# Two-layer graph attention on one core: the products of the score's last chunk alternated with the first transposes of layer 0

## The chip, the cores and the metric

The kernel runs on one core of one Trainium2 chip (trn2). Its engines are TensorE (PE in the profile; its weight loads are the row PEld), VectorE (DVE), ScalarE (ACT), GpSimd (POOL) and SyncE (SP), which here only issues DMAs. The metric is the device time of one execution in microseconds (us), as the median of several runs.

## What is computed

Layer 0 is a graph attention layer with a rank-one score and a cut, layer 1 a masked attention over fixed keys. Each is followed by a residual and a layer norm. There are 4096 nodes with 128 features, and `adj` is a 4096 x 4096 integer matrix.

```
# layer 0
h = x @ W
e = leaky_relu((h @ a_src)[:, None] + (h @ a_dst)[None, :], 0.2)
valid = (adj > 0) & (h.sum(axis=1) != 0)[None, :]
att = softmax(where(valid, e, -1e9), axis=1); att = where(valid, att, 0)
L = valid.sum(axis=1); top = att.max(axis=1)
attention = where(att >= 1e-4, att, 0) * L[:, None]
attention = where((top > 1e-4)[:, None], attention, 0)
x = layernorm(x + elu(h + attention @ h))
# layer 1
scores = leaky_relu(x @ ks.T, 0.2)
attn = softmax(where(adj > 0, scores, -9e15), axis=1)
out = layernorm(x + attn @ ks)
```

## The kernel before

The 4096 rows are worked off in 32 tiles of 128 rows. A tile's attention matrix is 128 x 4096, cut into four chunks of 1024 columns, and each chunk into eight blocks of 128. The loop is skewed: slot t does layer 0 of tile t and most of layer 1 of tile u = t - 1. There is no scheduler; each engine has its own instruction list written out by hand, in which semaphores (`pe.wait_ge(name, value)`, `.then_inc(name, 1)`) order it against the others.

TensorE's list for one slot (`slot(t)` in the tensor block) is, in this order:

- `score(u, 3)`: the fourth chunk of layer 1's score, six f16 products of 512 columns (lines 286, 287, 291). q and k are split into a high and a low f16 part; for each of the two banks there are high x high, high x low and low x high.
- `turn0(t, 0..3)`: 32 transposes of 128 x 128 f32 (line 211), eight per chunk, of layer 0's attention `att0`. The block of `att0` is the loaded operand, the identity is streamed.
- `sum0(t, 0..3)`: attention @ h, 32 f32 products that the trace shows as 64 matmuls (line 307).
- `turn1(u, 0..3)` and `sum1(u, 0..3)`: the same for layer 1 (lines 211 and 326), with `turn_q(t)` (line 332) between the second and the third sum. It transposes the new x to make q.
- `score(t, 0..2)`: the first three chunks of the next score.

Scores and transposes all go to `work`, a PSUM tensor of three slots of 1024 columns. Chunk c of a score uses slot c % 3, so the fourth uses slot 0 again; `turn0` uses the slots 1, 2, 0, 1. What a slot held must be read out by ScalarE before it is written again:

- `bend1(u, c)` (ScalarE, line 400) reads score chunk c, applies the leaky relu, writes `att1` and counts `bent1`.
- `copy0(t, c)` (ScalarE, line 394) copies the transposed chunk c to `att0T` and counts `copied0`.
- `score(u, 3)` waits for `bent1` of chunk 0 (value 4u + 1). `turn0(t, 0)`, `(t, 1)`, `(t, 2)` wait for `bent1` of chunks 1, 2, 3 (values 4u + 2, 4u + 3, 4u + 4). `turn0(t, 3)` waits for `copied0` of chunk 0. All four also wait for `cut_done`, the count of the cut of layer 0's attention by VectorE (line 516), and name that wait first.

ScalarE's list around this place is `bend1(u, 2)`, `bend1(u, 3)`, `copy0(t, 0..3)`, `raise1(u, 0)` (exponential of layer 1, line 405), `raise0(t + 1, 0)` (line 387), `raise1(u, 1)`, `copy1(u, 0)` (line 412) and on; `bend1(t, 0)` and `bend1(t, 1)` end the slot. VectorE applies the mask to each bent chunk (`mask1`, line 570), takes the row maximum (line 576), builds the next mask (line 477) and does the small steps that lead to the new x (line 561).

Of the kernel before, what the change touches and what calls it, by code (L numbers as in the profile page):

```python
# [5 lines left out]
P = 128  # L6
CHUNK = 1024
BANK = 512
# [19 lines left out]
def graph_layers(nc, x, adj, W, a, ks, out):  # L28
# [4 lines left out]
    CHUNKS = N // CHUNK  # L33
    PER = CHUNK // P
# [8 lines left out]
    with ExitStack() as ctx:  # L43
        def sb(name, shape, dt=F32):
            return ctx.enter_context(nc.sbuf_tensor(name, shape, dt))

        def pair(name, shape, dt=F32):
            return [sb(f"{name}{i}", shape, dt) for i in range(2)]

        def sem(name):  # L50
            return ctx.enter_context(nc.semaphore(name))

        def sem2(name):
# [4 lines left out]
        att0 = pair("att0_", [P, N])  # L58
# [6 lines left out]
        kT = sb("kT", [P, 2, N], F16)  # L65
# [9 lines left out]
        ident = sb("ident", [P, P])  # L75
# [35 lines left out]
        qT = sb("qT", [P, 2, P], F16)  # L111
# [7 lines left out]
        work = ctx.enter_context(nc.psum_tensor("work", [P, SLOTS, CHUNK], F32))  # L119
# [24 lines left out]
        z0_summed, cut0_ready, rz0_ready, cut_done = sem("z0_summed"), sem("cut0_ready"), sem("rz0_ready"), sem("cut_done")  # L144
        edges_ready, gate0_ready, coef0_ready = sem("edges_ready"), sem("gate0_ready"), sem("coef0_ready")
        turned0, copied0, summed0 = sem("turned0"), sem("copied0"), sem("summed0")
# [6 lines left out]
        scored, bent1, masked1, bias1_ready, exp1 = (  # L153
            sem("scored"), sem("bent1"), sem("masked1"), sem("bias1_ready"), sem("exp1"))
# [53 lines left out]
        def _(pe):  # L208
            def turn(n, c, source):
                for b in range(PER):  # L210
                    mm = pe.transpose(work[:, n % SLOTS, b * P:(b + 1) * P], source(c * PER + b), ident[:, :])  # L211
                return mm
# [19 lines left out]
            for c in range(CHUNKS):  # L232
# [4 lines left out]
                for b in range(CHUNK // BANK):  # L237
                    lo = c * CHUNK + b * BANK
                    mm = pe.matmul(work[:, (HT_AT + c) % SLOTS, b * BANK:(b + 1) * BANK], w_sb[:, :],  # L239
                                   xT[:, lo:lo + BANK], start=True, stop=True)  # L240
# [32 lines left out]
            def score(t, c):  # L273
                if c == 0:
                    pe.wait_ge(q_high, t + 1)
                    pe.wait_ge(q_low, t + 1)
                if c == 3:
                    pe.wait_ge(bent1, 4 * t + 1)
                elif t > 0:
                    pe.wait_ge(copied1, 4 * (t - 1) + c + 2)  # L280
                else:
                    pe.wait_ge(copied0, 4)
                for b in range(CHUNK // BANK):
                    part = slice(c * CHUNK + b * BANK, c * CHUNK + (b + 1) * BANK)
                    o = work[:, c % SLOTS, b * BANK:(b + 1) * BANK]
                    pe.matmul(o, qT[:, 0, :], kT[:, 0, part], start=True, stop=False)  # L286
                    pe.matmul(o, qT[:, 0, :], kT[:, 1, part], start=False, stop=False)  # L287
                for b in range(CHUNK // BANK):
                    part = slice(c * CHUNK + b * BANK, c * CHUNK + (b + 1) * BANK)
                    o = work[:, c % SLOTS, b * BANK:(b + 1) * BANK]  # L290
                    mm = pe.matmul(o, qT[:, 1, :], kT[:, 0, part], start=False, stop=True)  # L291
                mm.then_inc(scored, 1)

            def turn0(t, c):
                pe.wait_ge(cut_done, 2 * t + 1 + c // 2)
                if c == 3:
                    pe.wait_ge(copied0, 4 * t + 1)
                elif t > 0:
                    pe.wait_ge(bent1, 4 * (t - 1) + c + 2)
                turn((1, 2, 0, 1)[c], c, lambda b: att0[t % 2][:, b * P:(b + 1) * P]).then_inc(turned0, 1)  # L300

            def sum0(t, c):
                pe.wait_ge(copied0, 4 * t + c + 1)
                if c == 0 and t > 0:
                    pe.wait_ge(y_ready, t)
                for k in range(c * PER, (c + 1) * PER):
                    mm = pe.matmul(acc0, att0T[:, k * P:(k + 1) * P], h_all[:, k, :], start=(k == 0),  # L307
                                   stop=(k == BLOCKS - 1))
                mm.then_inc(summed0, 1)

            def turn1(u, c, layer0):
                pe.wait_ge(exp1, 2 * u + 1 + c // 2)
                if c == 3:
                    pe.wait_ge(copied1, 4 * u + 1)
                elif layer0:
                    pe.wait_ge(copied0, 4 * (u + 1) + c + 2)
                else:
                    pe.wait_ge(bent1, 4 * u + 4)
                turn((2, 0, 1, 2)[c], c, lambda b: att1[:, b * P:(b + 1) * P]).then_inc(turned1, 1)

            def sum1(u, c):
                pe.wait_ge(copied1, 4 * u + c + 1)
                if c == 0 and u > 0:
                    pe.wait_ge(res1_ready, u)
                for k in range(c * PER, (c + 1) * PER):
                    mm = pe.matmul(acc1, att1T[:, k * P:(k + 1) * P], k_all[:, k, :], start=(k == 0),  # L326
                                   stop=(k == BLOCKS - 1))
                mm.then_inc(summed1, 1)

            def turn_q(t):  # L330
                pe.wait_ge(x1_ready, t + 1)
                pe.transpose(qT_ps, x1[t % 2][:, :], ident[:, :]).then_inc(q_turned, 1)

            def slot(t):
                layer0, layer1, u = t < TILES, t > 0, t - 1
                if layer1:
                    score(u, 3)
                if layer0:
                    for c in range(CHUNKS):
                        turn0(t, c)  # L340
                    for c in range(CHUNKS):
                        sum0(t, c)
                if layer1:
                    for c in range(CHUNKS):
                        turn1(u, c, layer0)
                    sum1(u, 0)
                    sum1(u, 1)
                if layer0:
                    turn_q(t)
                if layer1:  # L350
                    sum1(u, 2)
                    sum1(u, 3)
                if layer0:
                    for c in range(3):
                        score(t, c)

            for t in range(TILES + 1):
                slot(t)
# [353 lines left out]
```

## Time and profile before

| | |
|---|---|
| median of 3 runs | 949.72 us (949.38 to 950.56) |
| the profiled execution, its own time | 949.38 us |
| its span in the trace | 947.6 us |
| TensorE's mean granted clock over the span | 0.977 |

One execution was profiled. The span runs from the first to the last instruction of the program; the execution's time is 1.8 us more. In the profile, a group of instructions has its line in the program, its engine, what it writes and reads, how many there are, the time the engine was busy with them and the mean length of one. Matmuls are pipelined: a matmul's record is longer than the distance to the next one, so what a stream of them costs is read from the distances, not from the lengths. The granted clock is 1.00 at 2.4 GHz and 0.50 at 1.2 GHz.

### The profile page before, as it was taken

The numbers are of one execution on the slowest core, as the hardware profiler recorded it, in microseconds if no ns is written. First come the engines' busy times: TensorE is split into PE (matmuls) and PEld (weight loads), VectorE is DVE, ScalarE is ACT, GpSimd is POOL, SyncE is SP. The second block draws the span as 40 slices with busy tenths as digits, with TensorE's granted clock in tenths as the row PEclk, the third lists the DMA queues.
The fourth block names the chain that finished last, engine by engine and source line by source line (L and its number), as shares of the span: only waits on it lengthen the run. The fifth ranks groups of instructions, "written<-read, shape, count | busy, mean of one in ns | idle before, by whom it ended". The sixth has DMA issues, their size and how long they took to land.

```text
span 947.6 us, 17708 instructions
## 1 busy us (share of the span) xinstructions
PE 907.8 (96%) x7152; PEld 802.8 (85%) x7152; DVE 753.2 (79%) x1231; ACT 779.9 (82%) x793; POOL 52.0 (5%) x136
## 2 busy tenths in 40 slices
PE   7954999999999999999999999999999999999996
PEld 4744888888899888888899888888899888888895
DVE  1575888888888898888888898888888898888422
ACT  4345989888898988988898898988898899988754
POOL 0000000000000000000000000000000000000000
PEclk9777999999999999999999999999999999999998
DMA  8204212222222112222222112222222112220000
GB/s 274 68 21 138 93 44 95 95 95 95 96 93 91 48 61 90 95 95 95 96 92 95 56 56 84 95 96 95 95 95 93 67 43 85 95 96 7 4 3 7
DMA packets 19537, 76.70 MB, mean 81 GB/s; under 512 B 1920, under 2 KB 14336, under 8 KB 15360
## 3 DMA queue, kind: packets, MB, share of 16 engines
q1 hardware_dynamic: 19456, 75.57, 22.7%
q8 instruction: 57, 0.93, 0.4%
q14 instruction: 24, 0.20, 0.1%
HBM read 73.47 MB, written 2.10 MB: 80 GB/s over the span
## 4 chain that ended last, share of the span: by engine, by line
PE 92%; DVE 3%; DMA 2%; issue 1%; ACT 1%; SPq 0%; POOL 0%; POOLq 0%; DVEq 0%; ACTq 0%
PE work L211 24%; PE bank L326 24%; PE bank L307 23%; PE work L286 6%; PE work L287 6%; PE work L291 6%; DMA adj_sb<-adj 2%; DVE att L488 1%; PE work L217 1%; PE work L218 1%; PE work L239 1%; DVE adj_sb L483 1%; DMA att<-x 1%; DVE mask L477 0%; ACT att L387 0%
## 5 line engine op out<-in xcount | busy, mean ns | idle before, releaser
L211 PE MATMUL work<-ident,att 128*128 128x128 f32 x2080 | 246.2, 278 | 20.7 <-ACT att0T L394 8.3
L211 PEld LDWEIGHTS work<-ident,att 128*128 128x128 f32 x2080 | 237.1, 143 | 28.4 <-issue 13.9
L326 PE MATMUL bank<-k_all,att1T 128*128 128x128 f32 x2048 | 237.3, 275 | 0.0
L307 PE MATMUL bank<-h_all,att0T 128*128 128x128 f32 x2048 | 235.1, 276 | 0.0
L326 PEld LDWEIGHTS bank<-k_all,att1T 128*128 128x128 f32 x2048 | 233.6, 192 | 0.0
L307 PEld LDWEIGHTS bank<-h_all,att0T 128*128 128x128 f32 x2048 | 232.5, 193 | 0.0
L570 DVE CUSTOM_DVE_ANT_0 att<-att,mask 128x1024 f32<-128x1024 f32 x128 | 156.8, 1225 | 28.0 <-ACT att L400 22.0
L400 ACT ACTIVATE att<-work 128x1024 f32<-128x1024 f32 x128 | 131.1, 1024 | 33.5 <-PE work L291 33.5
L412 ACT COPY att1T<-work 128x1024 f32<-128x1024 f32 x128 | 126.2, 1012 | 30.7 <-PE work L211 30.7
L516 DVE SCALAR_TENSOR_TENSOR att<-att,cut 128x2048 f32<-128x2048 f32 x64 | 147.4, 2345 | 0.0
L488 DVE CUSTOM_DVE_ANT_0 att<-adj_sb,d_all 128x4096 f32<-128x4096 bf16 x32 | 141.6, 4425 | 1.1
L380 ACT ACTIVATE att<-att,s_all 128x4096 f32<-128x4096 f32 x32 | 119.1, 3722 | 14.9 <-DVE top L488 14.9
L405 ACT ACTIVATE att<-att,bias 128x2048 f32<-128x2048 f32 x64 | 130.0, 2033 | 1.5 <-DVE bias L576 1.5
L387 ACT ACTIVATE att<-att,bias 128x2048 f32<-128x2048 f32 x64 | 129.0, 2016 | 0.0
L394 ACT COPY att0T<-work 128x1024 f32<-128x1024 f32 x128 | 120.3, 1036 | 0.3 <-PE work L211 0.3
L286 PE MATMUL work<-kT,qT 128*128 128x512 f16 x256 | 97.8, 382 | 0.7 <-ACT qT L422 0.7
L287 PE MATMUL work<-kT,qT 128*128 128x512 f16 x256 | 97.8, 382 | 0.0
L477 DVE TENSOR_SCALAR mask<-adj_sb 128x4096 bf16<-128x4096 int32 x32 | 73.4, 2294 | 25.5 <-DMA adj_sb<-adj 25.2
L291 PE MATMUL work<-kT,qT 128*128 128x512 f16 x256 | 76.6, 381 | 0.0
L483 DVE TENSOR_TENSOR adj_sb<-mask,zero_cols 128x4096 bf16<-128x4096 bf16 x32 | 73.0, 2283 | 0.0
L291 PEld LDWEIGHTS work<-kT,qT 128*128 128x128 f16 x256 | 25.2, 98 | 30.5 <-issue 0.5
L286 PEld LDWEIGHTS work<-kT,qT 128*128 128x128 f16 x256 | 25.3, 99 | 27.9 <-ACT qT L422 1.0
(69 smaller groups left out, 442.4 us busy)
## 6 DMA issues: line engine op xcount, KB each, us to landing
adj_sb<-adj SPq DMA_DIRECT2D x32, 2048.0 KB, 8.5
att<-x SPq DMA_DIRECT2D x4, 512.0 KB, 5.8
x_sb<-x SPq DMA_DIRECT2D x32, 64.0 KB, 7.4
out<-x SPq DMA_DIRECT2D x32, 64.0 KB, 1.5
w_sb<-W SPq DMA_DIRECT2D x1, 64.0 KB, 3.7
a_sb<-a SPq DMA_DIRECT2D x2, 0.5 KB, 3.6
k_all<-ks SPq DMA_DIRECT2D x1, 0.5 KB, 15.7
```

What stands on the lines that cost most here:

```text
L211: mm = pe.transpose(work[:, n % SLOTS, b * P:(b + 1) * P], source(c * PER + b), ident[:, :])
L286: pe.matmul(o, qT[:, 0, :], kT[:, 0, part], start=True, stop=False)
L287: pe.matmul(o, qT[:, 0, :], kT[:, 1, part], start=False, stop=False)
L291: mm = pe.matmul(o, qT[:, 1, :], kT[:, 0, part], start=False, stop=True)
L307: mm = pe.matmul(acc0, att0T[:, k * P:(k + 1) * P], h_all[:, k, :], start=(k == 0), stop=(k == BLOCKS - 1))
L326: mm = pe.matmul(acc1, att1T[:, k * P:(k + 1) * P], k_all[:, k, :], start=(k == 0), stop=(k == BLOCKS - 1))
L387: nc.scalar.activation(b, b, ACT.Exp, bias=bias0[f % 2][:, :], accum_out=z0[f % 2][:, k:k + 1]).then_inc(exp0, 1)
L400: nc.scalar.activation(att1[:, cols(c)], work[:, c % SLOTS, :], ACT.Prelu, alpha=SLOPE).then_inc(bent1, 1)
L405: nc.scalar.activation(att1[:, half(k)], att1[:, half(k)], ACT.Exp, bias=bias1[u % 2][:, :], accum_out=z1[u % 2][:, k:k + 1]).then_inc(exp ...
L488: nc.vector.tensor_tensor_reduce(att0[p][:, :], mask_and_zero, d_all[:, :], 1.0, -NO_ROW_MAX, ALU.add, ALU.max, top0[p][:, :]).then_inc(ma ...
L516: nc.vector.scalar_tensor_tensor(b, b, cut0[p][:, :], b, ALU.is_ge, ALU.mult).then_inc(cut_done, 1)
L570: nc.vector.tensor_tensor_reduce(att1[:, cols(c)], att1[:, cols(c)], mask[u % MASKS][:, cols(c)], 1.0, -3.0e38, ALU.add, ALU.max, top1[u % ...
```

## The change

In the slots that have both layers (t = 1 to 31), `score(u, 3)` and `turn0(t, 0)` are replaced by one function, `score_and_turn0(u, t)`. It first waits for `bent1` of chunk 1 (4u + 2) and for `cut_done`, and then issues the six products of the score's fourth chunk and the eight transposes of layer 0's first chunk in turn: product, transpose, product, transpose, and after the sixth pair the last two transposes. `scored` is counted by the sixth product, `turned0` by the eighth transpose. Slots, operands and the number of instructions are the same. The first and the last slot, with one layer only, keep the old order.

```diff
+            def score_and_turn0(u, t):
+
+                pe.wait_ge(bent1, 4 * u + 2)
+                pe.wait_ge(cut_done, 2 * t + 1)
+                for i in range(PER):
+                    if i < 4:
+                        b, k_part = i // 2, i % 2
+                        part = slice(3 * CHUNK + b * BANK, 3 * CHUNK + (b + 1) * BANK)
+                        pe.matmul(work[:, 0, b * BANK:(b + 1) * BANK], qT[:, 0, :], kT[:, k_part, part],
+                                  start=(k_part == 0), stop=False)
+                    elif i < 6:
+                        b = i - 4
+                        part = slice(3 * CHUNK + b * BANK, 3 * CHUNK + (b + 1) * BANK)
+                        mm = pe.matmul(work[:, 0, b * BANK:(b + 1) * BANK], qT[:, 1, :], kT[:, 0, part],
+                                       start=False, stop=True)
+                        if b == 1:
+                            mm.then_inc(scored, 1)
+                    mm = pe.transpose(work[:, 1, i * P:(i + 1) * P], att0[t % 2][:, i * P:(i + 1) * P], ident[:, :])
+                mm.then_inc(turned0, 1)
+
             def slot(t):
                 layer0, layer1, u = t < TILES, t > 0, t - 1
-                if layer1:
+                if layer1 and layer0:
+                    score_and_turn0(u, t)
+                elif layer1:
                     score(u, 3)
-                if layer0:
-                    for c in range(CHUNKS):
+                else:
+                    turn0(t, 0)
+                if layer0:
+                    for c in range(1, CHUNKS):
                         turn0(t, c)
                     for c in range(CHUNKS):
                         sum0(t, c)
```

TensorE's list before, from the last products of the score's third chunk to the end of `turn0` (L286, L287 and L291 are the score's products, L211 the transposes, `att_0` the buffer of layer 0's attention; the names in brackets are the semaphores waited for):

```order
142 L291 MATMUL work<-kT,qT 128x512 x2
143 L211 MATMUL work<-ident,att_0 128x128 [waits bent1,cut_done]
144 L211 MATMUL work<-ident,att_0 128x128 x7
145 L211 MATMUL work<-ident,att_0 128x128 [waits bent1,cut_done]
146 L211 MATMUL work<-ident,att_0 128x128 x7
147 L211 MATMUL work<-ident,att_0 128x128 [waits bent1,cut_done]
148 L211 MATMUL work<-ident,att_0 128x128 x7
149 L211 MATMUL work<-ident,att_0 128x128 [waits copied0,cut_done]
150 L211 MATMUL work<-ident,att_0 128x128 x7
```

Row 142 ends the fourth chunk of the score; the four chunks of transposes stand behind it, each with a wait at its first instruction. The same place of the changed kernel (L310 and L315 are now the fourth chunk's products, L319 the transposes between them):

```order
143 L310 MATMUL work<-kT,qT 128x512 [waits cut_done,bent1]
144 L319 MATMUL work<-ident,att_0 128x128
145 L310 MATMUL work<-kT,qT 128x512
...
151 L315 MATMUL work<-kT,qT 128x512
152 L319 MATMUL work<-ident,att_0 128x128
153 L315 MATMUL work<-kT,qT 128x512
154 L319 MATMUL work<-ident,att_0 128x128 x3
155 L211 MATMUL work<-ident,att_0 128x128 [waits bent1,cut_done]
156 L211 MATMUL work<-ident,att_0 128x128 x7
157 L211 MATMUL work<-ident,att_0 128x128 [waits bent1,cut_done]
158 L211 MATMUL work<-ident,att_0 128x128 x7
159 L211 MATMUL work<-ident,att_0 128x128 [waits copied0,cut_done]
160 L211 MATMUL work<-ident,att_0 128x128 x7
```

The score's last product (row 153) now has five transposes ahead of it that stood behind it, and the wait for `bent1` of chunk 1 stands ahead of the fourth chunk's first product. The lists of the other engines are the same as before.

## Rows read from the trace of the kernel before

**Rows 1.** The page: the span, busy engines, and the chain that ended last.
```profile
span 947.6 us, 17708 instructions
PE 907.8 (96%) x7152; PEld 802.8 (85%) x7152; DVE 753.2 (79%) x1231; ACT 779.9 (82%) x793; POOL 52.0 (5%) x136
PE 92%; DVE 3%; DMA 2%; issue 1%; ACT 1%; SPq 0%; POOL 0%; POOLq 0%; DVEq 0%; ACTq 0%
```

**Rows 2.** Busy time by stage: stretch, busy us (count) by engine, PEclk, DMA.
```profile
110.00:927.00 817.00, 815.55 (x6654) 728.42 (x6653) 687.38 (x1146) 715.65 (x730) 48.74 (x122) 1.00 0.22 78
35.00:36.70 1.70, 1.70 (x17) 1.70 (x17) 1.67 (x2) 0.00 (x0) 0.00 (x0) 1.00 0.00 0
54.00:57.00 3.00, 3.00 (x16) 3.00 (x15) 2.16 (x3) 1.31 (x2) 0.00 (x0) 0.50 0.00 0
38.00:43.00 5.00, 5.00 (x25) 5.00 (x25) 4.43 (x5) 1.06 (x1) 0.00 (x0) 0.50 0.15 26
```

**Rows 3.** Chain that ended last, one slot: start us, us, what.
```profile
442.12 0.21 PE work L286
...
447.31 3.49 PE work L211 x32
450.80 7.15 PE bank L307 x64
...
468.69 0.22 PE work L286
```

**Rows 4.** Timeline of PE, score's fourth chunk to first transposes: start us, us, engine line.
```profile
445.85 0.38 PE L286 MATMUL work<-kT,qT 128*128 128x512 f16 x1
...
446.71 0.59 PE L291 MATMUL work<-kT,qT 128*128 128x512 f16 x2
447.14 3.66 PE L211 MATMUL work<-ident,att 128*128 128x128 f32 x32
```

**Rows 5.** Timeline of ACT in the same place (the last row from a narrower window).
```profile
444.75 1.02 ACT L400 ACTIVATE att<-work 128x1024 f32<-128x1024 f32 x1 [0.27 <-PE work L291]
447.34 1.03 ACT L400 ACTIVATE att<-work 128x1024 f32<-128x1024 f32 x1 [0.27 <-PE work L291]
448.26 3.76 ACT L394 COPY att0T<-work 128x1024 f32<-128x1024 f32 x4
455.85 2.02 ACT L405 ACTIVATE att<-att,bias 128x2048 f32<-128x2048 f32 x1
458.86 1.01 ACT L412 COPY att1T<-work 128x1024 f32<-128x1024 f32 x1 [0.90 <-PE work L211]
...
448.26 1.01 ACT L394 COPY att0T<-work 128x1024 f32<-128x1024 f32 x1
```

**Rows 6.** Weight loads by kind: xcount | busy us, mean ns; first at full, then at half clock.
```profile
L222 PEld LDWEIGHTS bank<-a_sb,att0T 128*128 128x128 f32 x14 | 1.6, 192 | 0.0
L211 PEld LDWEIGHTS work<-ident,att 128*128 128x128 f32 x28 | 3.1, 140 | 0.2
...
L222 PEld LDWEIGHTS bank<-a_sb,att0T 128*128 128x128 f32 x25 | 5.5, 333 | 0.0
L211 PEld LDWEIGHTS work<-ident,att0T 128*128 128x128 f32 x9 | 1.9, 230 | 0.0
```

**Rows 7.** Timeline of PEld in 35.0:36.6 (products of one column), and the chain in 22:31.
```profile
34.88 1.87 PEld L222 LDWEIGHTS bank<-a_sb,att0T 128*128 128x128 f32 x16
...
24.08 0.86 PE work L217 x2
```

**Rows 8.** Timeline: two places where PE waited for a copy of ACT.
```profile
60.58 0.99 ACT L432 COPY h_all<-work 128x1024 f32<-128x1024 f32 x1
61.63 0.98 PE L211 MATMUL work<-ident,att0T 128*128 128x128 f32 x7 [2.45 <-ACT h_all L432]
...
75.99 0.99 ACT L394 COPY att0T<-work 128x1024 f32<-128x1024 f32 x1
77.12 0.66 PE L211 MATMUL work<-ident,att 128*128 128x128 f32 x2 [8.35 <-ACT att0T L394]
```

**Rows 9.** Timeline of DVE in 436:450.
```profile
437.02 0.35 DVE L561 TENSOR_SCALAR x<-res,mv,rstd 128x128 f32<-128x128 f32 x1 [0.99 <-POOL rstd L680]
439.09 4.61 DVE L516 SCALAR_TENSOR_TENSOR att<-att,cut 128x2048 f32<-128x2048 f32 x2
449.75 2.29 DVE L477 TENSOR_SCALAR mask<-adj_sb 128x4096 bf16<-128x4096 int32 x1
```

**Rows 10.** Timeline of PEld in 438:443.5, the transpose of q between the sums.
```profile
438.17 0.14 PEld L332 LDWEIGHTS bank<-ident,x 128*128 128x128 f32 x1
438.28 3.65 PEld L326 LDWEIGHTS bank<-k_all,att1T 128*128 128x128 f32 x32
441.85 0.10 PEld L286 LDWEIGHTS work<-kT,qT 128*128 128x128 f16 x1
441.96 0.10 PEld L287 LDWEIGHTS work<-kT,qT 128*128 128x128 f16 x1
```

## Prediction

> **What bounds the kernel now.** I read the page first: TensorE is busy 96% of the span and holds 92% of the chain that ended last [rows 1]. Then busy time by stage: from 110 to 927 us TensorE has no gap worth the name (815.55 of 817 us) and the full clock, 1.00, or 2.4 GHz [rows 2]. The chain over one slot shows only TensorE and a period of 468.69 - 442.12 = 26.57 us [rows 3]. So only what TensorE spends, or a wait that it does not have yet, can move the time, and whatever is gained or lost comes 31 times, in the slots 1 to 31.
>
> The next view is the timeline around the place of the change, to see how close the others are behind TensorE. The fourth chunk's first product starts at 445.85 [rows 4]; `bend1` of chunk 1 ended at 444.75 + 1.02 = 445.77 [rows 5], 0.08 earlier. The fourth chunk's last product ends at 446.71 + 0.59 = 447.30 [rows 4]; ScalarE starts `bend1` of chunk 3 at 447.34, ends it at 448.37, starts the first copy 0.92 after it began, at 448.26, and ends that copy at 449.27 [rows 5]. The transposes start at 447.14, 0.109 apart (3.49 / 32) [rows 3, 4]; so `turn0` chunk 2 starts at 448.89 and chunk 3 at 449.76. Chunk 2 needs the `bend1` that ended at 448.37 (0.52 earlier), chunk 3 the copy that ended at 449.27 (0.49 earlier). These are the margins that the change eats into.
>
> **The change part by part.**
>
> *Instructions.* None is added or dropped: six products at 0.216 (5.19 us from 442.12 to 447.31 for the 24 of a slot) and eight transposes at 0.109 [rows 3]. The question is whether they cost less side by side, that is, whether a transpose's 0.109 is its streaming or its weight load. Were it the load, it could hide under a product. A one-column f32 product streams nearly nothing, and still its loads stand (1.87 - 0.19) / 15 = 0.112 apart [rows 7], so a load of that kind can alone hold TensorE this long. But that load's record has 192 ns and a transpose's has 140, 52 less; at half clock they have 333 and 230, 103 less [rows 2, 6]. A difference that doubles with the clock is array work: about 0.05 less than the other's 0.11, so a transpose's load needs about 0.06. Its streaming is bounded by f32 products of 512 columns, 0.43 each [rows 7], or 0.107 for 128 columns: the 0.109 seen. I take the transposes as bound by streaming, with the load hidden already. Then pairing saves nothing, and all 14 instructions take 6 x 0.216 + 8 x 0.109 = 2.17 as before. The bounds are 0.056 and 0.109 for a transpose between products.
>
> The Trainium skill, page "TensorE: Matmul & The Clock Gate", section "LDWEIGHTS (loading the stationary operand)", gives a weight load as its columns divided by 1.2 GHz, whatever the type. By that, 128 columns take an estimated 107 ns, the transposes would be bound by loads, and the change would be a gain; that is the first rival below. The three lengths of load records in this trace, two of them for f32, speak against one price for all.
>
> *Switching.* A transpose among f32 products costs nothing extra: its load at 438.17, the next at 438.28; and the first f16 load at 441.85 is followed by the next at 441.96, one f32 step later [rows 10]. From f16 products to a transpose, 447.14 follows 446.93 (446.71 + 0.216) as one product does another [rows 4]. Only a transpose followed by an f16 product is not shown. Zero is the nearest rows' value; the upper bound is a load record left bare, 0.10, a gain has nothing to come from.
>
> *The wait moved ahead of the fourth chunk.* It asks for the `bend1` that ends at 445.77. How long does a release take? Where a transpose waited for one thing, it is recorded at 61.63, 0.05 to 0.06 after the copy's end at 61.57; its seven rows then run 0.05 long for 0.109 steps, so the array was held some 0.11 [rows 8]. Where the second of two waits held it, it came at 77.12, 0.14 after 76.98, and 0.17 by the distance to its second [rows 8]. Here `bent1` is named first and `cut_done` second, and `cut_done` is met: both cuts ended at 443.70 [rows 9]. The one-wait row is nearest, and an f16 load is about 0.04 shorter than a transpose's (0.10 against 0.14 [rows 6, 10]). That puts the product at 445.77 + 0.11 - 0.04 = 445.84, just in time; I take 0.02 late. Bounds: 0, and 445.77 + 0.17 = 445.94, or 0.09. Queued behind this wait is all of TensorE's list.
>
> *The five transposes ahead of the last product.* `scored` comes 5 x 0.109 = 0.55 later. Who waits: ScalarE, which was idle before this `bend1` anyhow. It now starts at 447.89 and ends at 448.92; the first copy starts at 448.81 and ends at 449.82. `turn0` chunk 2 would start at 448.89, but needs 448.92 plus a release. In `turn0` the wait for `bent1` or `copied0` is the second named, as in the 77.12 row, so I take 0.17: 449.09, which is 0.20 late. Chunk 3 is then due at 449.96 and released at 449.82 + 0.17 = 449.99, instead of 449.76: **0.23 lost**. After it the sums ask for copies that are ready, and TensorE keeps this lag. In short: 0.55 later against a cover of 0.49 - 0.17 = 0.32. Bounds of the release: 0.05 gives 449.87, or 0.11 lost; 0.17 gives 0.23.
>
> *What hides the rest.* ScalarE runs 0.55 late from here, but idles 0.90 before the copy at 458.86 [rows 5], which takes it up. Its second exponential, ended at 457.87, is not asked for before the third chunk of layer 1's transposes, two chunks (1.75) after 450.80 + 7.15 = 457.95 [rows 3]: 0.55 fits. VectorE's mask and row maximum of chunk 3 come 0.55 later, and so its mask at 449.75 [rows 9] and the new x. That x ended at 437.37, and the load that needs it came at 438.17 [rows 9, 10], 0.80 later; 0.55 - 0.25 uses 0.30 of it. SP's and POOL's lists are not touched, and no DMA moves.
>
> *The sum.* 0.23 + 0.02 = 0.25 per slot, times 31 = 7.8 us. The profiled execution's own time is 949.38, which gives 957.1; from the median, 0.34 higher, it would be 957.5. I forecast 957.3. The case's own ends are 0.11 x 31 = 3.4 (952.8) and (0.23 + 0.09) x 31 = 9.9 (959.3, or 959.6 from the median).
>
> **The rivals.**
>
> 1. *Loads bound the transposes, and pairing hides them: faster.* For it: the one-column loads at 0.112 [rows 7], so near 0.109. Against it: the load records and the 512-column products. A transpose between products would cost 0.056 or so (0.109 less 0.053). But `scored` would still come 5 x 0.056 = 0.28 later, and the first copy would end at 449.55. With a release of 0.17 chunk 3 starts at 449.72, a gain of 0.04; with 0.11, at 449.66, a gain of 0.10. So even then TensorE's 0.32 saved is mostly waited away: 1.2 to 3.1 us, 948.2 to 946.3, say 947.2. It decides the sign where five transposes cost less than the 0.32 of cover, 0.064 each.
>
> 2. *Cover is larger than I think: no change.* ScalarE's release of TensorE would have to be quick (0.05) and most of a transpose hidden (0.07 to 0.08 each), so that 0.55 becomes under 0.44. Time about 949.7.
>
> 3. *Each step from transpose to f16 product costs extra: much slower.* For it: no row shows that step. Against it: every other switch is free [rows 4, 10]. At up to 0.10 each, the last product comes 5 x 0.10 later still: 0.25 + 0.50 = 0.75 per slot, 23 us, 972.6; half of it gives 965.
>
> **How the numbers follow.** A measurement of this kernel can tell about 0.2%, or 1.9 us. My forecast has 0.77, rival 1 has 0.10, rival 2 has 0.04 and rival 3 has 0.09. The range is the forecast's own, 952.8 to 959.6, widened by a little below and to 962 above for the small end of rival 3: 952.5 to 962.0, leaving out some 2 in 10. Faster has most of rival 1, 0.09; same has the rest of it and rival 2, 0.05; slower has 0.86.
>
> **What would show it.** In the changed trace each product and transpose of the mixed stretch should take 0.325 a pair; 0.27 would prove rival 1, over 0.33 rival 3. TensorE should have gaps before the transposes of chunk 2 (about 0.20) and chunk 3 (about 0.03), released by lines 400 and 394 as numbered before (24 more in the changed kernel), and nearly none before the first product of the mix. ScalarE should start the fourth `bend1` some 2.04 after the first product of the mix instead of 1.49, and its idle time before the copy of layer 1 should shrink by about 0.3. The slot's period should be 26.82 instead of 26.57, the clock still 1.00. If the period is right but the gap stands at the first product, my split of it is wrong; if the new x holds TensorE, the cover that I named is gone; a period of 26.57 or less makes the forecast wrong.

## The result, and the profile after

| | before | changed |
|---|---|---|
| median | 949.92 us (948.36 to 950.56, 6 runs) | 956.69 us (955.14 to 957.86, 6 runs) |
| ratio to before | | 1.0073, 95% interval 1.006 to 1.0086 |
| the profiled execution, its own time | 949.38 us | 955.14 us |
| its span | 947.6 us | 953.4 us |

The kernel became slower by 0.73%. The page of the changed kernel looks like that of before [rows 1]; TensorE is as busy as it was, and the chain is still its own:

```profile
span 953.4 us, 17708 instructions
PE 912.3 (96%) x7152; PEld 801.6 (84%) x7152; DVE 752.9 (79%) x1231; ACT 780.4 (82%) x793; POOL 52.0 (5%) x136
PE 92%; DVE 3%; DMA 2%; issue 1%; ACT 1%; SPq 0%; POOL 0%; POOLq 0%; DVEq 0%; ACTq 0%
```

Busy time by stage, the stretch of [rows 2], says the same: the full clock (1.00), and seemingly no gap in TensorE.

```profile
110.00:927.00 817.00, 816.80 (x6627) 727.13 (x6626) 682.73 (x1139) 712.01 (x726) 48.72 (x122) 1.00 0.22 78
```

This view hides the loss: a matmul's record is 0.27 us long and the next normally starts 0.11 after it, so a gap of up to 0.16 disappears under the record before it. The number of instructions is a rough sign, 6627 matmuls in the same 817 us where there were 6654; it depends on where the window cuts the slots. The distances show the loss. Here is the chain over one slot, as in [rows 3] (L319, L310 and L315 are the mixed stretch, L352 is the transpose of q):

```profile
448.05 0.22 PE work L310
448.27 0.11 PE work L319
448.38 0.22 PE work L310
...
449.89 0.33 PE work L319 x3
450.22 0.87 PE work L211 x8
451.09 0.01 issue
451.10 1.97 PE work L211 x16
453.07 7.15 PE bank L327 x64
...
474.85 0.22 PE work L310
```

The period is 474.85 - 448.05 = 26.80 us instead of 26.57. A pair takes 448.38 - 448.05 = 0.33, the sum of its parts (0.216 + 0.109). The last three transposes of the mixed stretch end at 450.22, which is 2.17 after 448.05, just as the 14 instructions took before. The next 24 transposes, the chunks 1 to 3, fill 450.22 to 453.07 = 2.85 us, where 24 x 0.109 = 2.62 would do. All of the 0.23 is there. The timeline tells where in these three chunks: TensorE from 451 to 452 us and from 452 to 453.2, then its weight loads around chunk 2 and before the first product of the mix.

```profile
450.82 1.34 PE L211 MATMUL work<-ident,att 128*128 128x128 f32 x9
451.78 1.29 PE L211 MATMUL work<-ident,att 128*128 128x128 f32 x10
...
450.17 0.69 PEld L211 LDWEIGHTS work<-ident,att 128*128 128x128 f32 x6
451.07 1.76 PEld L211 LDWEIGHTS work<-ident,att 128*128 128x128 f32 x16 [0.21 <-issue]
447.87 0.10 PEld L310 LDWEIGHTS work<-kT,qT 128*128 128x128 f16 x1 [0.31 <-ACT att L424]
```

Nine transposes in step fill 8 x 0.109 and one record of 0.27, together 1.15; the nine from 450.82, which cross from chunk 1 to chunk 2, fill 1.34, and so 0.20 too much. The ten from 451.78, which cross from chunk 2 to chunk 3, should fill 1.26 and fill 1.29, 0.03 too much. Before the change 32 in a row filled 3.66 without a gap [rows 4]. The loads show the first of the two gaps openly: the last load of chunk 1 starts at 450.71, the next one only at 451.07, after 0.21 of idle time.

Two more views of the timeline show what holds them, ScalarE first:

```profile
446.79 1.02 ACT L424 ACTIVATE att<-work 128x1024 f32<-128x1024 f32 x1 [0.27 <-PE work L291]
449.93 1.03 ACT L424 ACTIVATE att<-work 128x1024 f32<-128x1024 f32 x1 [0.81 <-PE work L315]
450.85 3.76 ACT L418 COPY att0T<-work 128x1024 f32<-128x1024 f32 x4
461.13 1.94 ACT L436 COPY att1T<-work 128x1024 f32<-128x1024 f32 x2 [0.57 <-PE work L211]
```

and TensorE with its loads and VectorE, at the places of [rows 4] and of [rows 9, 10]:

```profile
447.46 0.59 PE L291 MATMUL work<-kT,qT 128*128 128x512 f16 x2
447.89 0.38 PE L310 MATMUL work<-kT,qT 128*128 128x512 f16 x1
...
439.37 0.35 DVE L585 TENSOR_SCALAR x<-res,mv,rstd 128x128 f32<-128x128 f32 x1 [0.99 <-POOL rstd L704]
...
440.21 0.14 PEld L352 LDWEIGHTS bank<-ident,x 128*128 128x128 f32 x1
```

The first product of the mix starts 0.43 after the first of the two L291 (two steps of 0.216): nothing is lost at the wait that moved. It does hold the first load: the bend of chunk 1 ends at 446.79 + 1.02 = 447.81, the load comes 0.06 later, at 447.87, after 0.31 of idle time, and the product starts at 447.89, just when it was due. The fourth bend (L424) starts 449.93 - 447.89 = 2.04 after that product, where it was 1.49 [rows 4, 5]; ScalarE has idled 0.81 before, and the four copies (L418) follow it. This bend ends at 449.93 + 1.03 = 450.96, and the load that was held, at 451.07, comes 0.11 after it. Further on, ScalarE's idle time before the copy of layer 1 is 0.57 instead of 0.90 [rows 5], and the new x is ready at 439.72, 0.49 before the load that needs it, instead of 0.80 [rows 9, 10]. Both covers have shrunk by a third of a microsecond and both hold.

### The profile page after: what moved, and what is told of

The parts are those of the page before. It is cut to its first block, busy times and chain, and to the rows that moved or that the text cites. A ratio compares the mean times of both kernels' runs of the same rounds, so it can differ in the third digit from the quotient of the medians.

```text
span 953.4 us, 17708 instructions
## 1 busy us (share of the span) xinstructions
PE 912.3 (96%) x7152; PEld 801.6 (84%) x7152; DVE 752.9 (79%) x1231; ACT 780.4 (82%) x793; POOL 52.0 (5%) x136
## 4 chain that ended last, share of the span: by engine, by line
PE 92%; DVE 3%; DMA 2%; issue 1%; ACT 1%; SPq 0%; POOL 0%; POOLq 0%; DVEq 0%; ACTq 0%
PE bank L346 24%; PE bank L327 23%; PE work L211 22%; PE work L286 4%; PE work L291 4%; PE work L287 4%; PE work L319 3%; PE work L310 3%; DMA adj_sb<-adj 2%; PE work L315 1%; DVE att L512 1%; PE work L217 1%; PE work L218 1%; PE work L239 1%; DVE adj_sb L507 1%
## 5 line engine op out<-in xcount | busy, mean ns | idle before, releaser
L211 PE MATMUL work<-ident,att 128*128 128x128 f32 x1832 | 225.9, 280 | 20.0 <-ACT att0T L418 7.4
L211 PEld LDWEIGHTS work<-ident,att 128*128 128x128 f32 x1832 | 207.7, 144 | 30.0 <-issue 19.4
L424 ACT ACTIVATE att<-work 128x1024 f32<-128x1024 f32 x128 | 131.3, 1026 | 49.9 <-PE work L315 25.2
L418 ACT COPY att0T<-work 128x1024 f32<-128x1024 f32 x128 | 120.4, 1037 | 0.3 <-PE work L211 0.3
L286 PE MATMUL work<-kT,qT 128*128 128x512 f16 x194 | 74.1, 382 | 0.7 <-ACT qT L446 0.7
L287 PE MATMUL work<-kT,qT 128*128 128x512 f16 x194 | 74.0, 382 | 0.0
L291 PE MATMUL work<-kT,qT 128*128 128x512 f16 x194 | 58.2, 382 | 0.0
L319 PE MATMUL work<-ident,att 128*128 128x128 f32 x248 | 57.5, 273 | 0.0
L310 PE MATMUL work<-kT,qT 128*128 128x512 f16 x124 | 42.0, 379 | 0.0
```

The source lines that it names most:

```text
L418: nc.scalar.copy(att0T[:, cols(c)], work[:, (1, 2, 0, 1)[c], :]).then_inc(copied0, 1)
L424: nc.scalar.activation(att1[:, cols(c)], work[:, c % SLOTS, :], ACT.Prelu, alpha=SLOPE).then_inc(bent1, 1)
```

## The experiments

My theory was that the five transposes ahead of the last product delay `scored` by 0.55 us, that ScalarE's chain behind it covers 0.32 of this, and that the pairing itself changes nothing. The rivals were a cost of the moved wait, a cost of each switch between kinds, and transposes that are bound by their loads.

**The wait alone.** The function of the change, rewritten so that it takes its order from a string, in which P is the next product and T the next transpose. The change's own order would read `PTPTPTPTPTPTTT`. This run has the order of before, behind the change's wait; only the line of the string is shown:

```diff
+                for what in "PPPPPPTTTTTTTT":
```

> The change's function with the order of before: six products, then eight transposes, but with the wait for bent1 of chunk 1 ahead of the products. My theory (the loss comes from the five transposes ahead of the last product): no loss, period 26.57 us, about 949.8 us. Rival (the early wait costs): up to 0.09 us per slot, period 26.66, about 952.5 us, with a gap before the first product.

Measured: 950.17 us median of 10 runs, ratio 1.0003 (0.9994 to 1.0013). The chain's transpose of q (L353), in two slots that follow each other:

```profile
464.72 0.11 PE bank L353
491.29 0.11 PE bank L353
```

The period is 491.29 - 464.72 = 26.57. The moved wait costs nothing; both the 0.02 of the sum and its upper bound of 0.09 were too much.

**Two, four and eight transposes ahead of the last product.** This varies the delay of `scored` and keeps the rest. Three kernels, of which the one line that differs is shown:

```diff
+                for what in "PTPTPPPPTTTTTT":     (two)
+                for what in "PTPTPTPTPPTTTT":     (four)
+                for what in "PTPTPTPTPTTTTP":     (eight)
```

> Two transposes stand ahead of the last product, six behind it. My theory (a cover of 0.32 us, five transposes eat 0.55): 0.22 us of delay is covered, no loss, period 26.57, about 949.8 us, no gap before the transposes of chunks 2 and 3. Rival (every step from a transpose to a product costs 0.23 / 5 = 0.046 us): 0.09 per slot, period 26.66, about 952.7 us.

> Four transposes ahead of the last product. My theory: 0.44 - 0.32 = 0.12 us lost per slot, period 26.69, about 953.5 us. Rival (cost per step from transpose to product, four of them): 0.18 per slot, period 26.75, about 955.5 us.

> All eight transposes ahead of the last product, five of them alternated as in the change, three more before the sixth product. My theory: 0.87 - 0.32 = 0.55 us lost per slot, period 27.12, about 966.9 us. Rival (cost per step from transpose to product, five as in the change): period 26.80 as in the change, about 956.9 us.

Measured, with the period between two transposes of q (L353 in these kernels):

| transposes ahead | delay of `scored` | period | loss per slot | median, ratio to before |
|---|---|---|---|---|
| 2 | 0.22 | 26.57 | 0.00 | 949.14, 0.9997 (0.9988 to 1.0006) |
| 4 | 0.44 | 26.69 | 0.12 | 953.74, 1.0045 (1.003 to 1.006) |
| 5 (the change) | 0.55 | 26.80 | 0.23 | 956.69, 1.0073 (1.006 to 1.0086) |
| 8 | 0.87 | 27.13 | 0.56 | 966.41, 1.018 (1.0163 to 1.0197) |

The chain of the kernel with two ahead:

```profile
464.82 0.11 PE bank L353
491.39 0.11 PE bank L353
```

with four ahead:

```profile
466.79 0.11 PE bank L353
493.48 0.11 PE bank L353
```

and with eight ahead, where the chain itself turns to ScalarE:

```profile
445.96 0.11 PE bank L353
...
455.48 0.23 PE work L312
455.71 0.02 issue
455.73 1.03 ACT att L425
456.76 0.14 issue
456.90 1.98 PE work L211 x16
...
473.09 0.11 PE bank L353
```

The loss is the delay less about 0.32, and zero below it. A price per switch would have cost 0.09 with two ahead and no more with eight than with five. Both are refuted. The last rows show the mechanism openly: last product, bend (L425), 0.14 to the transposes of the chunks 2 and 3.

**The order of the two waits in `turn0`.** The changed kernel with the wait for `bent1` or `copied0` named first.

```diff
             def turn0(t, c):
-                pe.wait_ge(cut_done, 2 * t + 1 + c // 2)
                 if c == 3:
                     pe.wait_ge(copied0, 4 * t + 1)
                 elif t > 0:
                     pe.wait_ge(bent1, 4 * (t - 1) + c + 2)
+                pe.wait_ge(cut_done, 2 * t + 1 + c // 2)
```

> The changed kernel, but turn0 names its wait for bent1 or copied0 first and the one for cut_done second. My theory (a release through the second-named wait takes 0.17 us until the array runs, through the first-named one 0.11): the loss falls from 0.23 to 0.17 us per slot, period 26.74, about 1.9 us less than the change, 954.9 us. Rival (the release takes the same time in either place): period 26.80, about 956.8 us.

Measured: 954.56 us median of 5 runs, ratio 1.0055 (1.0041 to 1.0068). The chain's transpose of q, then the fourth bend and the loads behind it:

```profile
468.20 0.11 PE bank L352
494.94 0.11 PE bank L352
...
450.91 1.03 ACT L424 ACTIVATE att<-work 128x1024 f32<-128x1024 f32 x1 [0.81 <-PE work L315]
451.99 1.76 PEld L211 LDWEIGHTS work<-ident,att 128*128 128x128 f32 x16 [0.15 <-ACT att L424]
```

The period is 26.74, a loss of 0.17. In time the kernel is 2.1 us below the change's median; the two ratios' intervals overlap slightly, and it is the period that settles it. The load comes 451.99 - 451.94 = 0.05 after the end of the bend, where it came 451.07 - 450.96 = 0.11 after it in the changed kernel. So the 0.06 between the two ways of release that the sum used, from two rows of the start of the kernel, holds in the loop. It is worth something only where a release is what TensorE waits for: before the change it is not.

**Half of the load.** The kernel before, in which the eight transposes of layer 0's fourth chunk load 64 columns instead of 128; half of the rows of those blocks are left out.

```diff
-                turn((1, 2, 0, 1)[c], c, lambda b: att0[t % 2][:, b * P:(b + 1) * P]).then_inc(turned0, 1)
+                if c == 3:
+                    for b in range(PER):
+                        lo = (c * PER + b) * P
+                        mm = pe.transpose(work[0:P // 2, 1, b * P:(b + 1) * P], att0[t % 2][:, lo:lo + P // 2], ident[:, :])
+                    mm.then_inc(turned0, 1)
+                else:
+                    turn((1, 2, 0, 1)[c], c, lambda b: att0[t % 2][:, b * P:(b + 1) * P]).then_inc(turned0, 1)
```

> The kernel before, but the eight transposes of layer 0's fourth chunk load only 64 of their 128 columns, and so leave out half of the rows of those blocks; they still stream the 128 columns of the identity. My theory (a transpose is bound by its streaming): they stand 0.109 us apart as before, period 26.57, about 949.8 us. Rival (a transpose is bound by its load): some 0.056 apart, the period 0.3 to 0.4 shorter, about 938 to 940 us.

Measured: 950.25 us in its one run, so that the distances have to carry the reading. Its chain and its groups in one window (L303 is the narrow form):

```profile
448.12 2.62 PE work L211 x24
450.74 0.87 PE work L303 x8
```

```profile
L211 PEld LDWEIGHTS work<-ident,att 128*128 128x128 f32 x24 | 2.7, 140 | 0.2
L303 PEld LDWEIGHTS work<-ident,att 128*64 128x64 f32 x8 | 0.9, 111 | 0.0
```

Eight of them take 0.87, or 0.109 each, as with the full load, though the load's record is 29 ns shorter. A load that is shorter does not bring the transposes closer together. The mixed stretch says the same: there each of the first six transposes has its load under a product of 0.216, and a pair still takes 0.216 + 0.109. So the transposes are not bound by their load. From the 29 ns for 64 columns one can estimate some 58 for 128, if every column costs the same; that is near the 0.06 that the prediction worked out from load records at two clocks.

**Transposes alternated with sums.** Each f32 product of a sum shows as two matmuls, called passes here. Since a pass takes 0.112 and a transpose 0.109, I looked for a gain of the kind that the change could not find.

```diff
+            def turn1_and_sum1(u):
+                pe.wait_ge(exp1, 2 * u + 2)
+                pe.wait_ge(copied1, 4 * u + 1)
+                if u > 0:
+                    pe.wait_ge(res1_ready, u)
+                for k in range(PER):
+                    b = 3 * PER + k
+                    mt = pe.transpose(work[:, 2, k * P:(k + 1) * P], att1[:, b * P:(b + 1) * P], ident[:, :])
...
+                    mm = pe.matmul(acc1, att1T[:, k * P:(k + 1) * P], k_all[:, k, :], start=(k == 0), stop=False)
...
-                    for c in range(CHUNKS):
+                    for c in range(3):
                         turn1(u, c, layer0)
-                    sum1(u, 0)
+                    turn1_and_sum1(u)
                     sum1(u, 1)
```

> The kernel before, with the transposes of layer 1's fourth chunk alternated with the eight products (sixteen passes) of the first sum instead of the f16 products. A sum's pass is bound by its load (0.112 apart), a transpose by its streaming (0.109), and nothing waits for the fourth chunk's copy for 4 us. My theory: no new wait, and a pass whose load stands under a transpose's streaming or the other way round takes 0.109 instead of 0.112: 0.02 to 0.04 us gained per slot, period 26.53 to 26.55, 0.6 to 1.2 us less than before. Rival (alternating kinds costs or the load stays bare): period 26.57 or more, 949.8 us or more.

Measured: 950.06 us median of 11 runs, ratio 1.0004 (0.9995 to 1.0013). The timeline of TensorE in the mixed stretch (L337 the transposes, L340 a product's two passes):

```profile
434.54 0.27 PE L337 MATMUL work<-ident,att 128*128 128x128 f32 x1
434.64 0.39 PE L340 MATMUL bank<-k_all,att1T 128*128 128x128 f32 x2
434.87 0.27 PE L337 MATMUL work<-ident,att 128*128 128x128 f32 x1
...
436.86 0.27 PE L337 MATMUL work<-ident,att 128*128 128x128 f32 x1
```

Seven rounds take 436.86 - 434.54 = 2.32, or 0.331 each, which is 0.109 + 2 x 0.111: nothing is gained, and the expectation was wrong. The rounds alone do not tell which of the three steps are the long ones. The starts in the trace do, taken over all slots of the loop: from a transpose to the pass behind it 109.1 ns on average (248 steps), from a pass to the next pass 111.7 (248), from a pass to a transpose 111.6 (217). A pass of a sum takes its 0.112 also where its load stands under a transpose, or where the next load is a transpose's short one. So the step of 0.112 is not set by the load of the next instruction. What sets it stays open; that a load of that kind bounds the passes was only argued from the one-column products [rows 7].

**A shorter chain on ScalarE.** TensorE's list stays mixed, with five transposes ahead of the last product, but bank 0 gets its three products first, and ScalarE bends the fourth chunk in two halves. VectorE's mask waits for both. The main lines:

```diff
+                products = ((0, 0, 0), (0, 0, 1), (0, 1, 0), (1, 0, 0), (1, 0, 1), (1, 1, 0))
...
+                        if n == 3:
+                            mm.then_inc(scored_half, 1)
...
+            def bend1_halves(u):
+                for k in range(2):
+                    if k == 0:
+                        act.wait_ge(scored_half, u + 1)
+                    else:
+                        act.wait_ge(scored, 4 * u + 4)
+                    if u > 0:
+                        act.wait_ge(turned1, 4 * u)
+                    lo = 3 * CHUNK + k * BANK
+                    nc.scalar.activation(att1[:, lo:lo + BANK], work[:, 0, k * BANK:(k + 1) * BANK], ACT.Prelu,
+                                         alpha=SLOPE).then_inc(bent_half if k == 0 else bent1, 1)
```

> All five transposes stand ahead of the last product as in the change, but bank 0 gets its three products first, and ScalarE bends the fourth chunk in two halves of 512 columns, the first as soon as bank 0 is scored. My theory (the loss is the chain last product, bend of chunk 3, first copy, transposes of chunk 3): the last product is followed by a half bend that ends some 0.4 us earlier, and by a copy that starts 0.4 us earlier, more than the 0.23 lost, so the period goes back to 26.57 and the time to about 949.8 us, though TensorE's list is as mixed as in the change. Rival (the mixed list itself holds TensorE): period 26.80, about 956.9 us.

Measured: 949.3 us median of 10 runs, ratio 0.9999 (0.999 to 1.0009). ScalarE's timeline (L440 the halves, L422 the copies), and the chain's two transposes of q:

```profile
449.14 0.60 ACT L440 ACTIVATE att<-work 128x512 f32<-128x512 f32 x1 [0.33 <-PE work L313]
449.63 3.76 ACT L422 COPY att0T<-work 128x1024 f32<-128x1024 f32 x4
```

```profile
466.26 0.11 PE bank L356
492.83 0.11 PE bank L356
```

The copies start 0.49 after the last half bend begins; with the whole bend it was 0.92. And the period is 26.57 again. So the loss is that chain and not the mixed list; beside the chain only the order of the products within the mix differs from the change. It also shows the limit: with the chain shortened the mixed order only equals the old one. No version here beats the kernel before by more than can be measured.

## Why the prediction was right

The forecast was 957.3 us (952.5 to 962.0), slower; the median came at 956.69. Its steps, one by one:

- *Pairing saves nothing.* Right: 2.17 us for the 14 instructions, and neither half a load nor a load under a product brought the transposes closer together. The first rival fell on both. That it is the streaming that spaces them stays an argument from the 512-column products [rows 7]. The Trainium skill, page "TensorE: Matmul & The Clock Gate", section "LDWEIGHTS (loading the stationary operand)", prices a load by its columns at 1.2 GHz; by that, 64 columns are worth an estimated 53 ns. The load records here differ by 29 (140 against 111) and disagree with it.
- *Switching costs nothing.* Right, also for the one step that no row had shown, from a transpose to an f16 product: a pair is 0.33, and eight ahead cost by the delay, not by switches.
- *The moved wait.* It was put at 0.02 late and cost nothing; this is the largest miss of the sum, 0.6 us of the total. It was near: the load came 0.06 after the end of the bend and only 0.02 ahead of its product.
- *The delay of `scored`.* 0.55 forecast; the bend started 2.04 after the first product, as forecast. Cover 0.32 forecast, and the runs with two, four, five and eight ahead give it back: 0.44 - 0.12, 0.55 - 0.23, 0.87 - 0.56, each 0.31 to 0.32.
- *Where the gap stands.* Right: 0.20 before chunk 2 and 0.03 before chunk 3 were forecast, and the transposes that cross into these chunks take 0.20 and 0.03 too long.
- *The price of the release.* Right, but on thin ground. The first transpose of chunk 2 counts from 450.82 + 0.11 + 0.20 = 451.13, which is the forecast 0.17 after the end of the bend at 450.96. The forecast's row at 77.12 [rows 8], though, stands behind 8.35 us of idle time where the granted clock is 0.50, or 1.2 GHz (76 to 78 us); the row at 61.63 with its 0.11 stands where it is 1.00, or 2.4 GHz (60 to 63 us). So the 0.06 between them could as well have come from the clock, and the prediction did not say so. Swapping the waits at the full clock took away just 0.06, and so it was the order of the waits; that the value read at half clock fitted the full one was partly luck.
- *The cover further on.* Right: both margins that were named shrank by about 0.3 and held.
- *The total.* 31 x 0.25 = 7.8 us forecast, 31 x 0.23 = 7.1 by the period, 6.8 between the medians. The profiled executions differ by only 5.8. From the first transpose of q to the last it was 916.5 - 93.7 = 822.8 before and 922.7 - 93.0 = 829.7 after, 6.9 more; ahead of the first the changed kernel was 0.7 shorter and behind the last 0.4. So the period is the sharper measure.

## What to carry to other kernels

When two kinds of instruction are to be alternated so that one hides the other's load, first ask whether the load is bare at all; halving it in a few instructions and reading their distances is a cheap test. Moving work ahead of an instruction that releases another engine delays that engine by all of it, and the margin to compare with is the last wait on the way back, less the time of a release. The busy time of matmuls did not show a gap that was shorter than a record; the period of the loop did, and so did the idle time in the row of the weight loads.

## What was not expected of the hardware

- A pass of an f32 sum took 0.112 us beside passes and beside transposes, 0.003 more than a transpose of the same width, also when its load stood under a transpose.
- The release of a waiting TensorE cost 0.06 us less when the late semaphore was named first of two: 26.80 against 26.74 us per slot. From the end of the bend to the load it was 0.11 us against 0.05. The start of the trace had hinted at it, at two different clocks [rows 8]; that it would hold so exactly in the loop was not expected.
